# The causal mask of the encoder's scores: from a matmul into PSUM to an addition on VectorE

## The chip, the cores and the metric

One core of one Trainium2 chip runs the whole program. The metric is the device time of one execution in microseconds, here as the median of several runs. The engines are named as in the profile: PE is TensorE (PEld its weight loads), DVE is VectorE, ACT is ScalarE, POOL is GpSimd, SP is SyncE, which issues the DMAs. Each engine works through its own queue in order; semaphores hold an instruction until another engine has done its part.

## The reference

Sixteen images of 37 tokens (36 patches and one class token) of width 256 go through a patch embedding, a block of causal attention with a mixture of experts, an encoder of six layers, and a feed-forward with 4-bit rounding. The change touches the attention of the six encoder layers, of which this matters:

```python
q_pos = jnp.arange(H, T + H)[:, None]
k_pos = jnp.arange(T + H)[None, :]
delta = q_pos - k_pos
valid = (delta >= 0) & (delta <= PAST_CTX)
...
for l in range(LAYERS):
    keys = jnp.concatenate([past, x], axis=1)
    ...
    scores = jnp.einsum('bqhd,bkhd->bhqk', q, k) / jnp.sqrt(jnp.asarray(HEAD_DIM, x.dtype))
    scores = jnp.where(valid[None, None], scores, neg)
    attn = jax.nn.softmax(scores, axis=-1)
    o = jnp.einsum('bhqk,bkhd->bqhd', attn, v).reshape(B, T, C)
```

With 16 heads of 16 columns each. The feed-forward of a layer is 256 to 1024 to 256 with a gelu, and the two layer norms stand behind the two residual additions.

## The kernel before

The images are handled in two halves of eight. In the encoder the two halves run half a layer apart: a stage `phase(x, y)` does the attention of one half (x) and, woven into it, the feed-forward of the other (y). There are twelve stages with attention: first (0, 0) alone, then six with the attention of half 1 beside the feed-forward of half 0 of the same layer, and between them five with the attention of half 0 of the next layer beside the feed-forward of half 1. Below, the first is called the lone stage, the six odd, the five even. All orders are written out by hand, one queue for each engine, and semaphores tie them together.

In an attention two images share one PSUM bank as a pair: a tile of 111 rows (3 x 37 queries) by 456 columns (2 images x 2 chunks x 3 heads x 38 keys). `scores` on TensorE (L825) fills it: one bf16 product of an identity with the mask, `amask` (L834), opens the bank and writes the mask into it, and four float32 products (L841) add the scores on top. VectorE then takes `row_max` from the bank (L2138) and `shift` subtracts it, from the bank into the probability tile `Pr` in SBUF (L2142), which frees the bank (`s_shifted`). ScalarE takes the exponent in place (L1545), VectorE the row sums (L2149) and their reciprocals (L2153), GpSimd multiplies (`normalise`, L1981), and TensorE transposes the result (L855) for the product with the values.

TensorE's order in a stage with both parts is: the transposed layer norm (L755), pairs 0 and 1, the first two hidden blocks of the feed-forward (L803), pair 2, two hidden blocks (L788), pair 3, four hidden blocks, the down products (L1330, 48 of them), the four sets of transposes (L855). Six PSUM banks go round in this order, so that each job waits for the job six places ahead of it (`free_bank`): the fourth hidden block uses the bank of pair 0, pair 3 that of pair 1, the seventh hidden block that of pair 2, the second half of the down products that of pair 3.

A hidden block goes through ScalarE (gelu, L1896, twice: in full and as a rounded high part `HF_H`). Its low part `HF_L`, the difference of the two, is made by VectorE for blocks 0 to 3 (`low_hidden`, L2722, `hl_ready`) and by GpSimd for blocks 4 to 7 (L2058). The down products of a block wait for its low part, in the order of the blocks. GpSimd also splits the layer's weights in the stages with y = (0, l) (L2000).

## Time and profile before

| | |
|---|---|
| median of 3 runs | 821.11 us (820.96 to 821.4) |
| span of the profiled execution, first to last instruction | 819.1 us |
| the profiled execution's own time | not listed; the median is 2.0 us above the span |
| PE, DVE, ACT, POOL busy | 98%, 77%, 56%, 31% of the span |
| granted TensorE clock | 1.000 over the whole span |
| mask products (L834), all / in the encoder | 56 / 48 |

The busy share of PE is that of pipelined matmuls, so a record is longer than the step from one matmul to the next. Times inside a stage are read from the timeline, which gives the start of each instruction in microseconds from the start of the span, its duration, and in brackets how long its engine stood idle before it and what ended that. Instructions of the same kind are merged, with their number behind an x.

### The profile page before, as it was taken

What the parts mean: (1) busy time and instruction counts of PE and PEld (TensorE: products, weight loads), DVE (VectorE), ACT (ScalarE), POOL (GpSimd) and SP (SyncE); (2) the same over time, 40 slices, a digit from 0 to 9 for tenths busy, and PEclk for the clock granted to TensorE, in tenths of its full rate; (3) what the DMA queues carried; (4) which work ended last, traced back from release to release, by engine and by line L of the source; (5) the groups of instructions that cost most, each with busy time, mean ns of one, the idle gap of its engine ahead of it and who ended that gap; (6) DMA issues with size and microseconds to landing.
All of it is one profiled execution on the core that took longest, in us unless ns stands there. A gap on an engine that the chain in (4) does not pass through costs nothing.

```text
span 819.1 us, 16629 instructions
## 1 busy us (share of the span) xinstructions
PE 801.5 (98%) x6060; PEld 751.4 (92%) x6060; DVE 633.9 (77%) x1287; ACT 460.6 (56%) x829; POOL 251.6 (31%) x297
## 2 busy tenths in 40 slices
PE   9999999999999999999999999999999999999988
PEld 8998789999999999899999989999998999999758
DVE  5786693778778876778797887878778787876796
ACT  4386424433333336585786777667687767745421
POOL 0002120410111100364366147335525623633020
PEclk9999999999999999999999999999999999999999
DMA  5010946998889812010210021031012103010001
GB/s 191 1 52 1 373 124 253 328 323 310 317 309 337 321 53 107 1 40 14 100 44 0 17 98 38 13 102 38 4 39 72 38 13 102 26 82 1 1 0 30
DMA packets 18290, 88.36 MB, mean 108 GB/s; under 512 B 3120, under 2 KB 7472, under 8 KB 12240
## 3 DMA queue, kind: packets, MB, share of 16 engines
q1 hardware_dynamic: 18256, 87.90, 30.4%
q8 instruction: 22, 0.36, 0.2%
q14 instruction: 12, 0.10, 0.0%
HBM read 85.05 MB, written 2.84 MB: 107 GB/s over the span
## 4 chain that ended last, share of the span: by engine, by line
PE 47%; issue 23%; POOL 18%; DVE 8%; ACT 3%; DMA 1%; POOLq 0%; SPq 0%; DVEq 0%; ACTq 0%
PE bank L1139 14%; POOL W_L L2000 7%; PE bank L1176 6%; POOL HF_L L2058 4%; POOL arena L1981 3%; POOL WQKV_L L2000 3%; PE bank L746 2%; PE bank L872 2%; PE bank L1185 2%; PE bank L722 2%; PE bank L1049 2%; PE bank L788 1%; POOL SQ L2019 1%; PE bank L1123 1%; PE bank L1490 1%
## 5 line engine op out<-in xcount | busy, mean ns | idle before, releaser
L1139 PE MATMUL bank<-arena 128*128 (+1 forms) x1024 | 117.8, 274 | 0.0
L1139 PEld LDWEIGHTS bank<-arena 128*128 128x128 f32 x1024 | 117.4, 192 | 0.0
L1981 POOL TENSOR_TENSOR arena<-arena,srec 111x456 f32<-111x456 f32 x56 | 52.3, 962 | 125.1 <-DVE srec L2153 125.1
L2000 POOL TENSOR_TENSOR W_L<-LW,W_H 128x256 fp32r<-128x256 f32 x96 | 68.5, 752 | 36.9 <-DVE XHL L2589 33.5
L2058 POOL TENSOR_TENSOR HF_L<-arena,HF_H 128x296 fp32r<-128x296 f32 x48 | 43.8, 937 | 76.7 <-ACT HF_H L1896 76.7
L788 PE MATMUL bank<-XHL,W_H 128*128 128x296 f32 x288 | 65.1, 307 | 0.0
L1896 ACT ACTIVATE arena<-bank,vec 128x296 f32<-128x296 f32 x96 | 48.8, 509 | 20.4 <-PE bank L788 15.4
L2012 POOL TENSOR_TENSOR QW<-QW,arena x14 | 22.4, 1600 | 119.0 <-DVE QW L2490 65.6
L1330 PE MATMUL bank<-HF_L,W_H 128*128 128x296 f32 x192 | 57.4, 299 | 0.0
L1330 PE MATMUL bank<-HF_H,W_H 128*128 128x296 f32 x192 | 57.4, 299 | 0.0
L1330 PE MATMUL bank<-HF_H,W_L 128*128 128x296 f32 x192 | 57.3, 299 | 0.0
L872 PE MATMUL bank<-arena 114*128 114x111 f32 x448 | 55.1, 276 | 0.8 <-issue 0.7
L872 PEld LDWEIGHTS bank<-arena 114*128 114x128 f32 x448 | 53.1, 192 | 2.6 <-issue 1.3
L2165 DVE TENSOR_SCALAR OB<-bank,lvec 96x148 f32<-96x148 f32 x144 | 51.1, 368 | 5.7 <-PE bank L872 3.3
L841 PEld LDWEIGHTS bank<-arena 128*111 128x111 f32 x448 | 52.4, 175 | 1.1
L841 PE MATMUL bank<-arena 128*111 128x114 f32 x448 | 52.7, 260 | 0.0
L2149 DVE TENSOR_REDUCE ssum<-arena 111x12 f32<-111x456 f32 x56 | 32.1, 608 | 23.8 <-ACT arena L1545 23.6
L788 PEld LDWEIGHTS bank<-XHL,W_H 128*128 128x128 f32 x288 | 48.3, 188 | 0.3
L1896 ACT ACTIVATE HF_H<-bank,vec 128x296 fp32r<-128x296 f32 x96 | 48.3, 503 | 0.0
L788 PE MATMUL bank<-XHL,WQKV_H 128*128 128x296 f32 x192 | 45.4, 311 | 0.0
L2138 DVE TENSOR_REDUCE smax<-bank 111x12 f32<-111x456 f32 x56 | 33.9, 622 | 14.4 <-PE bank L841 14.3
L2497 DVE TENSOR_TENSOR EWD_L<-arena,EWD_H 128x2048 fp32r<-128x2048 f32 x16 | 36.9, 2304 | 10.0 <-ACT EWD_H L1758 10.0
(276 smaller groups left out, 2205.4 us busy)
## 6 DMA issues: line engine op xcount, KB each, us to landing
arena<-ew_in SPq DMA_DIRECT2D x16, 2048.0 KB, 9.0
arena<-ew_in SPq DMA_DIRECT2D x16, 1024.0 KB, 7.0
LW<-lw_in SPq DMA_DIRECT2D x12, 1024.0 KB, 5.0
arena<-route SPq DMA_DIRECT2D x32, 185.0 KB, 3.2
LW<-lw_in SPq DMA_DIRECT2D x6, 768.0 KB, 4.3
fp_weights<-arena SPq DMA_DIRECT2D x1, 2048.0 KB, 6.4
arena<-fp_weights SPq DMA_DIRECT2D x1, 2048.0 KB, 7.2
arena<-patches_in SPq DMA_DIRECT2D x2, 864.0 KB, 7.4
```

Of the source, the lines that this page charges most:

```text
L788: last = mm(o, w, x, start=(i == 0), stop=(i == len(pairs) - 1))
L841: last = mm(o[0:QROWS, col:col + KROWS], Qe[:, h, c, bb].rearrange("p s q -> p (s q)"), Ke[:, at_half(plan, h), c, bb].rearrange("p g k -> ...
L872: last = mm(o[:, i * QROWS:(i + 1) * QROWS], Ve[0:KROWS, at_half(plan, h) * HB + b % HB, c * P:(c + 1) * P], PTr[0:KROWS, b % PSLOTS, c, : ...
L1139: last = mm(o[:, m * CAP:(m + 1) * CAP], w[:, kc, mi * P:(mi + 1) * P], xg(kc, e), start=(kc == 0), stop=(kc == C - 1))
L1176: last = mm(bank[4][0:CAP, 0:D], hid_part, w_part, start=(m == 0 and i == 0), stop=(m == EM - 1 and i == 2))
L1330: last = mm(bank_of(plan, keys[c])[:, 0:NHALF], w, moving, start=(m == 0 and i == 0), stop=(m == FM - 1 and i == 2))
L1896: last = f(out[:, m, :], bank_of(plan, ("f1", FM * hy + m))[:, 0:NHALF], ACT.Gelu, bias=vec[:, 3 * C + m:3 * C + m + 1])
L1981: nc.gpsimd.tensor_tensor(v, v, srec[0:QROWS, s:s + 2, :].unsqueeze(3).to_broadcast([QROWS, 2, C * JH, KEYS]), ALU.mult).then_inc(p_ready, 1)
L2000: last = nc.gpsimd.tensor_tensor(low[:, cols], value[:, cols], high[:, cols], ALU.subtract)
L2058: nc.gpsimd.tensor_tensor(HF_L[:, m, :], HF[:, m, :], HF_H[:, m, :], ALU.subtract).then_inc(hl_ready_pool, 1)
L2165: return v.tensor_scalar(dst, src, bias(c)[lo:hi, :], None, ALU.add)
L2497: v.tensor_tensor(EWD_L[s][:, :, :], value, EWD_H[s][:, :, :], ALU.subtract).then_inc(wd_low, 1)
```

## The change

In the encoder (not in block 0) the mask product goes, and the first of the four score products of a pair opens the bank. VectorE gets a new step, `add_mask`: it reads the bank and the mask (in SBUF, bf16, the same for all heads) and writes the masked scores into `Pr`. It counts up a new semaphore `s_masked`, for which `free_bank` now waits in place of `s_shifted`. The max is then taken from `Pr` (`masked_max`) and subtracted in `Pr` in place (`masked_shift`). VectorE's order in the score block is written anew, and the low parts of hidden blocks 0 and 1 move inside it.

```diff
+                    if prev[0] == "s" and not plan.first:
+                        pe.wait_ge(s_masked, count_in(plan, prev, r, key) - PER_ROUND["s"])
-                    if needs is not None and needs[0] == prev[0]:
+                    elif needs is not None and needs[0] == prev[0]:
...
-                mm(o[0:QROWS, 0:2 * SCOLS], amask[:, 0:QROWS],
-                   amask[:, m0:m0 + KROWS].unsqueeze(1).to_broadcast([P, 2 * C, KROWS]), start=True, stop=False,
-                   skip_group_check=True)
+                if plan.first:
+                    mm(o[0:QROWS, 0:2 * SCOLS], amask[:, 0:QROWS],
+                       amask[:, P:P + KROWS].unsqueeze(1).to_broadcast([P, 2 * C, KROWS]), start=True, stop=False,
+                       skip_group_check=True)
...
+            def add_mask(r, plan, p):
+                dve.wait_ge(filled["s"], nth("s", p, r))
+                v.tensor_tensor(pair_probs(p).rearrange("p (x g) k -> p x (g k)", g=JH),
+                                bank_of(plan, ("s", p))[0:QROWS, 0:2 * SCOLS].rearrange("p (x n) -> p x n", n=KROWS),
+                                amask[0:QROWS, P + KROWS:P + 2 * KROWS].unsqueeze(1).to_broadcast([QROWS, 2 * C, KROWS]),
+                                ALU.add).then_inc(s_masked, 1)
+
+            def masked_max(r, p):
+                dve.wait_ge(s_masked, nth_enc("s", p, r))
+                v.tensor_reduce(pair_view(smax, p), pair_probs(p), AX.X, ALU.max).then_inc(s_max, 1)
+
+            def masked_shift(r, p):
+                dve.wait_ge(s_max, nth("s", p, r))
+                v.tensor_tensor(pair_probs(p), pair_probs(p),
+                                pair_view(smax, p).unsqueeze(2).to_broadcast([QROWS, 2 * C * JH, KEYS]), ALU.subtract
+                                ).then_inc(s_shifted, 1)
...
-                    for i in range(1, HB // 2):
-                        row_max(rx, plan, p0 + i)
-                        shift(rx, plan, p0 + i - 1)
-                        if y and i == 3:
-                            low_hidden(0, 1)
-                    shift(rx, plan, p0 + HB // 2 - 1)
+                    add_mask(rx, plan, p0)
+                    add_mask(rx, plan, p0 + 1)
+                    masked_max(rx, p0)
+                    masked_max(rx, p0 + 1)
+                    masked_shift(rx, p0)
+                    masked_shift(rx, p0 + 1)
...
```

The rest of the order can be seen in what VectorE's queue holds. The score block of a stage with both parts, before (`smax` is the tile of maxima, L2722 the low parts of hidden blocks 0 to 3):

```order
L2138 TENSOR_REDUCE smax<-bank 111x12 [waits s_psum] x2
L2142 TENSOR_TENSOR arena<-bank,smax 111x456 [waits s_max]
L2138 TENSOR_REDUCE smax<-bank 111x12 [waits s_psum]
L2142 TENSOR_TENSOR arena<-bank,smax 111x456 [waits s_max]
L2138 TENSOR_REDUCE smax<-bank 111x12 [waits s_psum]
L2142 TENSOR_TENSOR arena<-bank,smax 111x456 [waits s_max]
L2722 TENSOR_TENSOR HF_L<-arena,HF_H 128x296 [waits gelu_ready] x2
L2142 TENSOR_TENSOR arena<-bank,smax 111x456 [waits s_max]
L2722 TENSOR_TENSOR HF_L<-arena,HF_H 128x296 [waits gelu_ready] x2
L2149 TENSOR_REDUCE ssum<-arena 111x12 [waits p_exp] x2
```

And after the change, where L2142 is the masked add, L2149 the max, L2153 the shift, and L2743 the low parts:

```order
L2142 TENSOR_TENSOR arena<-bank,amask 111x456 [waits s_psum] x2
L2149 TENSOR_REDUCE smax<-arena 111x12 [waits s_masked] x2
L2153 TENSOR_TENSOR arena<-arena,smax 111x456 [waits s_max] x2
L2142 TENSOR_TENSOR arena<-bank,amask 111x456 [waits s_psum]
L2743 TENSOR_TENSOR HF_L<-arena,HF_H 128x296 [waits gelu_ready]
L2149 TENSOR_REDUCE smax<-arena 111x12 [waits s_masked]
L2142 TENSOR_TENSOR arena<-bank,amask 111x456 [waits s_psum]
L2153 TENSOR_TENSOR arena<-arena,smax 111x456 [waits s_max]
L2149 TENSOR_REDUCE smax<-arena 111x12 [waits s_masked]
L2743 TENSOR_TENSOR HF_L<-arena,HF_H 128x296 [waits gelu_ready]
L2153 TENSOR_TENSOR arena<-arena,smax 111x456 [waits s_max]
L2743 TENSOR_TENSOR HF_L<-arena,HF_H 128x296 [waits gelu_ready] x2
```

Four masked adds are new, the max and the shift read `arena` (the probability tile) and no bank, the low part of block 0 stands between the third add and the third max, that of block 1 between the fourth max and the fourth shift, and those of blocks 2 and 3 still behind all of them.

TensorE's queue around pair 3 of such a stage, before (L788 are the fourth and then the fifth hidden block):

```order
L788 MATMUL bank<-XHL,W_H 128x296 [waits s_shifted]
L788 MATMUL bank<-XHL,W_L 128x296
L788 MATMUL bank<-XHL,W_H 128x296
L788 MATMUL bank<-XHL,W_L 128x296
L788 MATMUL bank<-XHL,W_H 128x296 x2
L834 MATMUL bank<-amask 111x456 [waits s_shifted]
L841 MATMUL bank<-arena 111x114 x4
L788 MATMUL bank<-XHL,W_H 128x296 [waits gelu_ready]
```

After the change (L791 is the hidden block, L844 the score products):

```order
L791 MATMUL bank<-XHL,W_H 128x296 [waits s_masked]
L791 MATMUL bank<-XHL,W_L 128x296
L791 MATMUL bank<-XHL,W_H 128x296
L791 MATMUL bank<-XHL,W_L 128x296
L791 MATMUL bank<-XHL,W_H 128x296 x2
L844 MATMUL bank<-arena 111x114 [waits s_masked]
L844 MATMUL bank<-arena 111x114 x3
L791 MATMUL bank<-XHL,W_H 128x296 [waits gelu_ready]
```

The mask product is gone there, and the fourth hidden block and pair 3 wait for the masked add of pairs 0 and 1 and no longer for their shift.

The stage with attention alone has this on VectorE before, between the spread of the values and the row sums:

```order
L2138 TENSOR_REDUCE smax<-bank 111x12 [waits s_psum]
L2138 TENSOR_REDUCE smax<-bank 111x12 [waits s_psum,fp4_stored]
L2142 TENSOR_TENSOR arena<-bank,smax 111x456 [waits s_max]
L2138 TENSOR_REDUCE smax<-bank 111x12 [waits s_psum]
L2142 TENSOR_TENSOR arena<-bank,smax 111x456 [waits s_max]
L2138 TENSOR_REDUCE smax<-bank 111x12 [waits s_psum]
L2142 TENSOR_TENSOR arena<-bank,smax 111x456 [waits s_max] x2
L2149 TENSOR_REDUCE ssum<-arena 111x12 [waits p_exp] x2
```

After:

```order
L2142 TENSOR_TENSOR arena<-bank,amask 111x456 [waits s_psum,fp4_stored]
L2142 TENSOR_TENSOR arena<-bank,amask 111x456 [waits s_psum]
L2149 TENSOR_REDUCE smax<-arena 111x12 [waits s_masked] x2
L2153 TENSOR_TENSOR arena<-arena,smax 111x456 [waits s_max] x2
L2142 TENSOR_TENSOR arena<-bank,amask 111x456 [waits s_psum]
L2149 TENSOR_REDUCE smax<-arena 111x12 [waits s_masked]
L2142 TENSOR_TENSOR arena<-bank,amask 111x456 [waits s_psum]
L2153 TENSOR_TENSOR arena<-arena,smax 111x456 [waits s_max]
L2149 TENSOR_REDUCE smax<-arena 111x12 [waits s_masked]
L2153 TENSOR_TENSOR arena<-arena,smax 111x456 [waits s_max]
L2170 TENSOR_REDUCE ssum<-arena 111x12 [waits p_exp] x2
```

Eight instructions become twelve ahead of the first row sum (L2149 before, L2170 after).

## Rows read from the trace of the kernel before

**Rows 1.** Page, busy us (share of the span) and instructions of the engines:

```profile
PE 801.5 (98%) x6060; PEld 751.4 (92%) x6060; DVE 633.9 (77%) x1287; ACT 460.6 (56%) x829; POOL 251.6 (31%) x297
```

**Rows 2.** Line of the mask product: durations min/median/max ns; idle time before it:

```profile
L834 PE MATMUL bank<-amask x56: 353/356/402, 48.3 to 712.7; 128*111 128x456 bf16 x56
...
  DVE arena L2142: 1.3, 6
```

**Rows 3.** Timeline of TensorE (start us, duration us), odd stage, third and fourth mask:

```profile
639.28 0.35 PE L834 MATMUL bank<-amask 128*111 128x456 bf16 x1
639.48 0.94 PE L841 MATMUL bank<-arena 128*111 128x114 f32 x8
...
642.14 0.13 PEld L834 LDWEIGHTS bank<-amask 128*111 128x111 bf16 x1 [0.23 <-DVE arena L2142]
```

**Rows 4.** Timeline of VectorE, the same stage, [idle before <- what ended it]:

```profile
639.31 1.16 DVE L2138 TENSOR_REDUCE smax<-bank 111x12 f32<-111x456 f32 x2
640.39 0.62 DVE L2142 TENSOR_TENSOR arena<-bank,smax 111x456 f32<-111x456 f32 x1
...
643.36 0.63 DVE L2138 TENSOR_REDUCE smax<-bank 111x12 f32<-111x456 f32 x1 [1.27 <-PE bank L841]
...
649.49 1.16 DVE L2149 TENSOR_REDUCE ssum<-arena 111x12 f32<-111x456 f32 x2 [2.15 <-ACT arena L1545]
```

**Rows 5.** Timeline of GpSimd and VectorE, single instructions of the same stage:

```profile
638.27 4.22 POOL L2000 TENSOR_TENSOR W_L<-LW,W_H 128x256 fp32r<-128x256 f32 x6 [1.31 <-DVE XHL L2589]
...
645.17 0.83 POOL L2058 TENSOR_TENSOR HF_L<-arena,HF_H 128x296 fp32r<-128x296 f32 x1 [2.68 <-ACT HF_H L1896]
...
645.99 1.02 POOL L2058 TENSOR_TENSOR HF_L<-arena,HF_H 128x296 fp32r<-128x296 f32 x1
...
645.74 0.58 DVE L2722 TENSOR_TENSOR HF_L<-arena,HF_H 128x296 fp32r<-128x296 f32 x1
...
646.25 1.08 DVE L2722 TENSOR_TENSOR HF_L<-arena,HF_H 128x296 fp32r<-128x296 f32 x1
```

**Rows 6.** Timeline of GpSimd and VectorE, the lone stage, single instructions:

```profile
333.51 1.19 POOL L1981 TENSOR_TENSOR arena<-arena,srec 111x456 f32<-111x456 f32 x1
...
334.35 0.67 DVE L2576 TENSOR_TENSOR XD<-CN,const 128x296 f32<-128x296 f32 x1
```

**Rows 7.** Lines of VectorE: durations min/median/max ns, first and last start:

```profile
L2138 DVE TENSOR_REDUCE smax<-bank x56: 569/622/635, 49.8 to 714.0; 111x12 f32<-111x456 f32 x56
...
L2149 DVE TENSOR_REDUCE ssum<-arena x56: 568/616/628, 52.2 to 721.9; 111x12 f32<-111x456 f32 x56
...
L2722 DVE TENSOR_TENSOR HF_L<-arena,HF_H x48: 455/466/1086, 361.7 to 747.0; 128x296 fp32r<-128x296 f32 x48
```

**Rows 8.** Timeline of TensorE, odd stage, first down product and the transposes:

```profile
646.45 0.30 PE L1330 MATMUL bank<-HF_H,W_H 128*128 128x296 f32 x1
...
653.00 1.36 PE L855 MATMUL bank<-const,arena 111*114 111x111 f32 x12
654.70 0.57 PE L855 MATMUL bank<-const,arena 111*114 111x111 f32 x4 [0.34 <-POOL arena L1981]
```

**Rows 9.** Timeline of an even stage: VectorE, GpSimd, TensorE:

```profile
674.45 1.16 DVE L2138 TENSOR_REDUCE smax<-bank 111x12 f32<-111x456 f32 x2
...
680.32 3.62 POOL L2058 TENSOR_TENSOR HF_L<-arena,HF_H 128x296 fp32r<-128x296 f32 x4 [12.13 <-ACT HF_H L1896]
...
681.58 0.31 PE L1330 MATMUL bank<-HF_H,W_H 128*128 128x296 f32 x1
```

**Rows 10.** Timeline of the lone stage: VectorE, GpSimd:

```profile
326.54 0.63 DVE L2138 TENSOR_REDUCE smax<-bank 111x12 f32<-111x456 f32 x1 [0.30 <-PE bank L841]
...
330.33 1.15 DVE L2149 TENSOR_REDUCE ssum<-arena 111x12 f32<-111x456 f32 x2
...
331.69 4.14 POOL L1981 TENSOR_TENSOR arena<-arena,srec 111x456 f32<-111x456 f32 x4 [37.17 <-DVE srec L2153]
```

More of the change, by code:

```diff
@@ L430, in build @@
         q_ready, k_ready, v_ready, o_ready = (sem(n) for n in ("q_ready", "k_ready", "v_ready", "o_ready"))
+        s_masked = sem("s_masked")
         s_max, s_shifted, p_exp, s_sum, s_rec, p_ready, pt_ready = (
@@ L832, in scores @@
                 o = bank_of(plan, key)
-                m0 = P + (0 if plan.first else KROWS)
-                mm(o[0:QROWS, 0:2 * SCOLS], amask[:, 0:QROWS],
-                   amask[:, m0:m0 + KROWS].unsqueeze(1).to_broadcast([P, 2 * C, KROWS]), start=True, stop=False,
-                   skip_group_check=True)
+                if plan.first:
+                    mm(o[0:QROWS, 0:2 * SCOLS], amask[:, 0:QROWS],
+                       amask[:, P:P + KROWS].unsqueeze(1).to_broadcast([P, 2 * C, KROWS]), start=True, stop=False,
+                       skip_group_check=True)
                 for i in range(2):
@@ L841, in scores @@
                         last = mm(o[0:QROWS, col:col + KROWS], Qe[:, h, c, bb].rearrange("p s q -> p (s q)"),
-                                  Ke[:, at_half(plan, h), c, bb].rearrange("p g k -> p (g k)"), start=False, stop=True,
+                                  Ke[:, at_half(plan, h), c, bb].rearrange("p g k -> p (g k)"),
+                                  start=not plan.first and i + c == 0, stop=True,
                                   skip_group_check=True)
@@ L2752, in phase @@
                 if x:
-                    row_max(rx, plan, p0)
                     if isinstance(lx, int) and hx + lx == 0:
                         dve.wait_ge(fp4_stored, 32)
-                    for i in range(1, HB // 2):
-                        row_max(rx, plan, p0 + i)
-                        shift(rx, plan, p0 + i - 1)
-                        if y and i == 3:
-                            low_hidden(0, 1)
-                    shift(rx, plan, p0 + HB // 2 - 1)
+                    add_mask(rx, plan, p0)
[4 more added lines that the diff above has]
+                    masked_shift(rx, p0 + 1)
+                    add_mask(rx, plan, p0 + 2)
+                    if y:
+                        low_hidden(0)
+                    masked_max(rx, p0 + 2)
+                    add_mask(rx, plan, p0 + 3)
+                    masked_shift(rx, p0 + 2)
+                    masked_max(rx, p0 + 3)
+                    if y:
+                        low_hidden(1)
+                    masked_shift(rx, p0 + 3)
                     if y:
```

## The prediction

> **What bounds the kernel now.** I read the page first: TensorE is busy 98% of the span and VectorE 77% [rows 1]. So a matmul that goes is worth its slot, as long as nothing else then comes late. Next the mask product's own line: 56 of them, 356 ns each by the record, and a wait of 1.3 us in 6 cases for the shift of an earlier pair [rows 2]. The change keeps 8 of the 56 (block 0) and removes 48, four in each of twelve encoder stages: one lone, six odd, five even. Then the timeline of one odd stage: the score block on VectorE has a hole of 1.27 us ahead of the fourth max and one of 2.15 us ahead of the first row sum [rows 4]. That looks like room for the added work. The question is whether the rest of VectorE's queue, the low parts of the hidden blocks above all, still comes in time for TensorE.
>
> **What is removed.** Matmuls overlap, so the price is the step to the next start and not the 356 ns: 639.28 to 639.48, 0.20 us [rows 3]. Four make 0.80 us a stage; in odd stages the fourth score pair also waited 0.23 us for a shift [rows 3], which goes because the bank is now free at the masked add. So TensorE reaches its down products 1.03 us earlier in an odd stage and 0.8 us in an even one. Were that all, 6 x 1.03 + 6 x 0.8 = 11 us would go.
>
> **What is added on VectorE.** Four masked adds a stage, from PSUM with a mask in SBUF. No row shows one; the nearest are the shift from PSUM, 0.62 us also while GpSimd runs [rows 4], and the max and the row sum of the same size, 0.622 and 0.616 us [rows 7]. Back to back they start 0.54 us apart (two maxima from 639.31, the next instruction at 640.39 [rows 4]). I take 0.54; the bounds are 0.5 and 0.65. So max from SBUF costs what it cost from PSUM, and the block grows by 4 x 0.54 = 2.2 us.
>
> The Trainium skill, "VectorE: DVE Perf Modes", section on the TRN2 errata, gives 58 cycles of fixed cost from SBUF and 120 from PSUM, so max and shift would each be shorter by an estimated 0.065 us. The 0.616 beside 0.622 us do not show it [rows 7]. By the page the third shift would be issued some 0.3 us earlier, the even stages would lose nothing (see the race below) and the sum would be about 825.
>
> **The shift changes its kind.** It now reads two tensors in SBUF, as the low parts of L2722 do. Those take 0.46 us alone and up to 1.09 us [rows 7]. The row by row view says why: one is issued at 645.74 while GpSimd's first low part runs (645.17 to 646.00) and ends at 646.32; the next is issued at 646.25 and ends at 647.33, 0.32 us behind the end of GpSimd's second, which itself took 1.02 instead of 0.83 us [rows 5]. So the two take turns, whole instruction by whole instruction. An addition with a repeated second operand is held in the same way: issued at 334.35, it ends at 335.02, 0.32 us behind GpSimd's 333.51 + 1.19 [rows 6]. For 456 columns I scale: a held shift ends 0.32 x 456/296 = 0.49 us after GpSimd's instruction, and pushes the next one back by 0.19 + 0.17 = 0.36 us.
>
> The Trainium skill, "SBUF — State Buffer", section "SBUF: two separate sides", states this as an exclusive lock between GpSimd and VectorE instructions with two SBUF inputs. By it the masked shift is held and the masked add and the max are not; by that rule the trace agrees for two other operations [rows 5, 6]; none shows it for the shift itself.
>
> **An odd stage, worked out** (the times are those of the stage shown [rows 4]). Masked adds at 639.31 and 639.85, max at 640.39 and 640.93, first shift issued at 641.47. GpSimd splits weights until 642.49 in six of 0.70 us [rows 5]: the shift waits for the fifth (641.8) and ends at 642.3, the sixth moves to 642.87, the second shift ends at 643.36. Third add to 643.9, low part 0 to 644.28, third max, fourth add, third shift issued at 645.28. GpSimd's low parts, which follow the hidden blocks, start at 645.17 - 1.03 = 644.15 and end at 645.05 and 645.85, so the third shift ends at 646.34. Fourth max, low part 1 issued at 646.8: held by GpSimd's third (to 647.1), done at 647.4. Fourth shift held by GpSimd's fourth (to 648.1), done at 648.6. Low parts 2 and 3 at 648.95 and 649.35.
> TensorE: the seventh hidden block needs the bank of the third pair, masked at 643.9, and would start at 646.45 - 12 x 0.137 - 1.03 = 643.78, so it loses some 0.2 us; down starts at 646.45 - 1.03 + 0.2 = 645.6 (48 products in the 6.55 us to 653.00, 0.137 us each, 0.82 us a hidden block [rows 8]). Block 1 is wanted at 646.4 and its low part comes at 647.4: 1.0 us of waiting. Block 2 is wanted at 648.2, ready at 648.95: 0.75 us. Block 3 is in time. The transposes start at 653.00 - 0.83 + 1.75 = 653.9 instead of 653.00. Before, the fourth set waited for GpSimd's normalised tile and began at 654.70 [rows 8]; now the row sum starts at 649.4 (649.49 before [rows 4]), so that tile is no later and there is nothing to wait for: the fourth set begins some 1.2 us behind the first, 655.1. **Odd: +0.4 us each.**
>
> **An even stage.** GpSimd splits nothing in the score block. First add at 674.45 [rows 9], third shift issued at 679.68. GpSimd's low parts start at 680.32 - 0.8 = 679.52, so they win by 0.16 us. Shift to 680.84, low part 1 to 681.8, fourth shift to 683.0, low part 2 to 683.95. Down starts at 681.58 - 0.8 = 680.78 [rows 9]; block 1 waits 0.25 us, block 2 1.35 us. The transposes come 0.8 us later, the fourth set, relieved of its wait of about 0.5 us, **+0.3 us each**. If the shift won that race, low part 2 would be ready at some 683.4 and the stage would lose nothing.
>
> **The lone stage.** Here no feed-forward covers anything. VectorE runs without a pause from its second max (326.54, behind a hole of 0.30 us) to the row sum (330.33), and GpSimd, which releases the transposes, waits for it until 331.69 [rows 10]. Four more instructions less the hole: 4 x 0.54 - 0.3 = **+1.9 us**, all on the path. No GpSimd work stands beside it, so no shift is held.
>
> **Sum.** 1.9 + 6 x 0.4 + 5 x 0.3 = +5.8 us in the profiled execution, whose span is 819.1; the runs' median is 821.11, 2.0 above the span, and so what lies around the span is taken as unchanged and the difference is added to the median: 826.9. Bounds: no loss in even stages and 0.2 in odd ones gives +3.1 (824.2); 0.6 in both gives +8.5 (829.6).
>
> **The rivals.**
> *Faster: the ports do not hold the masked shift* (or GpSimd lets it by). Then low part 1 is ready before TensorE wants it and the waits in down vanish; the fourth transposes move with the gelus, by 1.0 us a stage: 11 x -1.0 + 1.9 = -9.1 us, 812. It decides from the point where low part 1 is done before 646.2 in the odd stage. For it: the shift from PSUM was never held [rows 4]. Against it: two instructions that were held, one with a repeated operand [rows 5, 6]. A part of it, low part 2 held but not 1, gives about 0.4 us less a stage than before, 817 to 819.
> *No change:* the even stages win the race and gain a little, the odd ones break even, and the lone stage alone is left: 821.1 + 1.9 less one or two, 821 to 822.7.
> *Much slower:* the low parts slip by one more GpSimd instruction (0.8 us) in every stage: 826.9 + 11 x 0.5 = 832.4.
>
> **How the numbers follow.** A measurement tells 0.2% (1.6 us) from no change. Forecast, 823 to 830: 0.58. Much slower: 0.07. Within 0.2%: 0.14. Faster: 0.21, of which 0.11 near 812 and 0.10 between 815 and 819. So faster 0.21, same 0.14, slower 0.65. The range for 8 in 10 leaves out the case near 812 and the far end above: 815 to 831; the forecast's own range is 823 to 830.
>
> **What would show it.** In the changed profile: 8 mask products on TensorE; masked shifts of about 0.6 us alone but 0.8 to 1.2 us beside GpSimd; TensorE waiting in the down products for HF_L of VectorE, about 1.7 us a stage; no wait of the fourth transposes for GpSimd; the lone stage's row sums 1.9 us later. I am wrong if shifts beside GpSimd stay at 0.62 us, or if no wait for HF_L appears in down.

## The result, and the profile after

The changed kernel takes 825.97 us (825.26 to 826.4, 4 runs) against 821.13 us before (820.96 to 821.4, 4 runs, the same chip): a ratio of 1.0054, 95% interval 1.004 to 1.0069. It is slower by 4.8 us; 826.9 was forecast.

The page's line of the engines, as [rows 1]. TensorE has 48 matmuls and 4.0 us of work less, VectorE 48 instructions and 28.8 us more:

```profile
PE 797.5 (97%) x6012; PEld 746.9 (91%) x6012; DVE 662.7 (80%) x1335; ACT 459.7 (56%) x829; POOL 260.6 (32%) x297
```

The new lines of VectorE and the low parts, as [rows 7] (durations min/median/max in ns, first and last start, forms). L2142 is the masked add, L2149 the max, L2153 the masked shift, L2743 the low part:

```profile
L2142 DVE TENSOR_TENSOR arena<-bank,amask x48: 618/623/630, 326.6 to 720.2; 111x456 f32<-111x456 f32 x48
...
L2149 DVE TENSOR_REDUCE smax<-arena x48: 614/617/628, 327.7 to 721.9; 111x12 f32<-111x456 f32 x48
...
L2153 DVE TENSOR_TENSOR arena<-arena,smax x48: 621/1116/1249, 328.8 to 722.9; 111x456 f32<-111x456 f32 x48
...
L2743 DVE TENSOR_TENSOR HF_L<-arena,HF_H x48: 450/455/546, 365.0 to 752.4; 128x296 fp32r<-128x296 f32 x48
```

Add and max hardly vary (by 12 and 14 ns). The shift does: 0.62 us at best, 1.12 in the median. The low parts, up to 1086 ns before [rows 7], are now at most 546: the shifts have taken over being held.

What TensorE waits for, in all (us, times, longest), on its weight loads first and then on the matmuls:

```profile
PEld bank L1334 <- DVE HF_L L2743: 15.5, 22, 1.1
```

```profile
PE bank L1334 <- DVE HF_L L2743: 9.6, 17, 0.9
PE bank L859 <- POOL arena L1985: 2.8, 2, 2.4
```

The first row is the new loss: the down products wait for VectorE's low parts, twice in each of the 11 stages that have them. It is read on the weight loads, because a matmul's record (0.30 us) is longer than the step to the next (0.137): the bracket behind a matmul begins at the end of that record and so shows less than was lost. The last row is the lone stage.

The odd stage, as [rows 4 and 5]: VectorE, then GpSimd (start, duration, xcount):

```profile
643.95 1.16 DVE L2142 TENSOR_TENSOR arena<-bank,amask 111x456 f32<-111x456 f32 x2
645.02 1.15 DVE L2149 TENSOR_REDUCE smax<-arena 111x12 f32<-111x456 f32 x2
646.09 1.94 DVE L2153 TENSOR_TENSOR arena<-arena,smax 111x456 f32<-111x456 f32 x2
...
649.95 1.10 DVE L2153 TENSOR_TENSOR arena<-arena,smax 111x456 f32<-111x456 f32 x1
650.98 0.62 DVE L2149 TENSOR_REDUCE smax<-arena 111x12 f32<-111x456 f32 x1
651.51 0.54 DVE L2743 TENSOR_TENSOR HF_L<-arena,HF_H 128x296 fp32r<-128x296 f32 x1
651.98 1.24 DVE L2153 TENSOR_TENSOR arena<-arena,smax 111x456 f32<-111x456 f32 x1
653.14 0.83 DVE L2743 TENSOR_TENSOR HF_L<-arena,HF_H 128x296 fp32r<-128x296 f32 x2
```

```profile
643.61 3.94 POOL L2004 TENSOR_TENSOR W_L<-LW,W_H 128x256 fp32r<-128x256 f32 x5
648.91 1.65 POOL L2062 TENSOR_TENSOR HF_L<-arena,HF_H 128x296 fp32r<-128x296 f32 x2 [1.36 <-ACT HF_H L1900]
650.74 1.98 POOL L2062 TENSOR_TENSOR HF_L<-arena,HF_H 128x296 fp32r<-128x296 f32 x2 [0.18 <-ACT HF_H L1900]
```

VectorE goes without a pause, but part of that is time in which GpSimd holds it: the third shift, issued at 649.95, ends at 651.05, 0.49 us behind GpSimd's second low part (650.56). The low part of block 1 comes at 652.05. TensorE's matmuls and weight loads of that stage, as [rows 8]:

```profile
650.38 0.30 PE L1334 MATMUL bank<-HF_H,W_H 128*128 128x296 f32 x1
...
658.66 1.68 PE L859 MATMUL bank<-const,arena 111*114 111x111 f32 x16
```

```profile
652.11 0.19 PEld L1334 LDWEIGHTS bank<-HF_H,W_H 128*128 128x128 f32 x1 [0.99 <-DVE HF_L L2743]
...
653.65 0.19 PEld L1334 LDWEIGHTS bank<-HF_H,W_H 128*128 128x128 f32 x1 [0.69 <-DVE HF_L L2743]
```

Block 1 waits 0.99 us and block 2 0.69; the down products take 658.66 - 650.38 = 8.28 us instead of 6.55 [rows 8]. All four sets of transposes then run as one group (x16), without the wait for GpSimd of [rows 8].

The even stage, as [rows 9]: VectorE, GpSimd's four low parts and the last two of them alone, TensorE's two waits and its transposes:

```profile
684.75 1.17 DVE L2153 TENSOR_TENSOR arena<-arena,smax 111x456 f32<-111x456 f32 x1
...
686.38 0.55 DVE L2743 TENSOR_TENSOR HF_L<-arena,HF_H 128x296 fp32r<-128x296 f32 x1
686.85 1.25 DVE L2153 TENSOR_TENSOR arena<-arena,smax 111x456 f32<-111x456 f32 x1
688.02 0.83 DVE L2743 TENSOR_TENSOR HF_L<-arena,HF_H 128x296 fp32r<-128x296 f32 x2
```

```profile
684.61 4.93 POOL L2062 TENSOR_TENSOR HF_L<-arena,HF_H 128x296 fp32r<-128x296 f32 x4 [11.35 <-ACT HF_H L1900]
...
686.56 1.04 POOL L2062 TENSOR_TENSOR HF_L<-arena,HF_H 128x296 fp32r<-128x296 f32 x1
...
687.57 1.97 POOL L2062 TENSOR_TENSOR HF_L<-arena,HF_H 128x296 fp32r<-128x296 f32 x1
```

```profile
686.98 0.19 PEld L1334 LDWEIGHTS bank<-HF_H,W_H 128*128 128x128 f32 x1 [0.36 <-DVE HF_L L2743]
...
688.53 0.19 PEld L1334 LDWEIGHTS bank<-HF_H,W_H 128*128 128x128 f32 x1 [0.70 <-DVE HF_L L2743]
```

```profile
693.54 1.69 PE L859 MATMUL bank<-const,arena 111*114 111x111 f32 x16
```

GpSimd wins the first race (684.61 against 684.75), as forecast. But its fourth low part, issued at 687.57 while the fourth shift is at work, takes 1.97 us: VectorE's low parts 2 and 3, next in its queue, go ahead of it, and low part 2 is done at 688.47. It was the other way round just before: the fourth shift was issued as closely behind low part 1 (at 686.85, with low part 1 ending at 686.93), and yet GpSimd's third low part (issued at 686.56, done at 687.60) came in between them, so that the shift ended at 688.10.

The lone stage, as [rows 10]: TensorE's first two sets of transposes, and its granted clock (the column behind the engines' busy times):

```profile
335.70 0.60 PE L859 MATMUL bank<-const,arena 111*114 111x111 f32 x4 [2.40 <-POOL arena L1985]
336.71 0.85 PE L859 MATMUL bank<-const,arena 111*114 111x111 f32 x4 [0.41 <-POOL arena L1985]
```

```profile
336.00:338.00 2.00, 1.59 (x11) 1.41 (x9) 1.93 (x6) 0.45 (x1) 2.00 (x3) 0.71 0.00 0
338.00:340.00 2.00, 2.00 (x12) 2.00 (x11) 1.54 (x3) 1.74 (x4) 0.84 (x1) 0.50 0.00 0
```

TensorE stands idle for 2.40 us, and behind that the clock falls to 0.50, the lower of its two levels (1.2 of 2.4 GHz), where it was 1.00 throughout before.

By stage, counted from the last transpose of one stage to the last of the next, and for the lone stage from its first score product (mask or score) to the first product with the values:

| us | before | after | difference | forecast |
|---|---|---|---|---|
| lone stage | 12.13 | 15.13 | +3.0 | +1.9 |
| odd stages, median of six | 35.58 | 36.00 | +0.4 (sum +2.4) | +0.4 (+2.4) |
| even stages, all five | 35.12 | 34.89 | -0.23 (sum -1.15) | +0.3 (+1.5) |

Together +4.25 us. The profiled execution also reached its first score product 1.0 us later. That is scatter: in the traces below, of kernels that leave the front of the program alone, that product starts between 324.5 and 325.4 us.

### The profile page after: what moved, and what is told of

It reads as the page before. It is cut to its first block, busy times and chain, and to the rows that moved or that the text cites. A ratio compares the mean times of both kernels' runs of the same rounds, so it can differ in the third digit from the quotient of the medians.

```text
span 824.5 us, 16651 instructions
## 1 busy us (share of the span) xinstructions
PE 797.5 (97%) x6012; PEld 746.9 (91%) x6012; DVE 662.7 (80%) x1335; ACT 459.7 (56%) x829; POOL 260.6 (32%) x297
## 4 chain that ended last, share of the span: by engine, by line
PE 62%; DVE 21%; issue 9%; POOL 5%; ACT 2%; DMA 1%; DVEq 0%; SPq 0%; POOLq 0%; ACTq 0%
PE bank L1143 14%; PE bank L1334 7%; PE bank L1180 6%; DVE arena L2153 3%; PE bank L747 3%; DVE smax L2149 3%; PE bank L791 3%; POOL W_L L2004 2%; PE bank L859 2%; PE bank L876 2%; DVE arena L2122 2%; PE bank L723 2%; PE bank L824 2%; PE bank L894 2%; DVE OB L2186 2%
## 5 line engine op out<-in xcount | busy, mean ns | idle before, releaser
L2004 POOL TENSOR_TENSOR W_L<-LW,W_H 128x256 fp32r<-128x256 f32 x96 | 70.9, 775 | 37.8 <-DVE XHL L2610 33.5
L2062 POOL TENSOR_TENSOR HF_L<-arena,HF_H 128x296 fp32r<-128x296 f32 x48 | 50.5, 1068 | 66.0 <-ACT HF_H L1900 65.9
L1334 PE MATMUL bank<-HF_H,W_H 128*128 128x296 f32 x192 | 59.7, 311 | 10.2 <-DVE HF_L L2743 9.6
L791 PE MATMUL bank<-XHL,W_H 128*128 128x296 f32 x288 | 65.8, 308 | 0.0
L844 PE MATMUL bank<-arena 128*111 128x114 f32 x448 | 51.2, 262 | 0.0
L1334 PEld LDWEIGHTS bank<-HF_H,W_H 128*128 128x128 f32 x192 | 36.1, 188 | 15.5 <-DVE HF_L L2743 15.5
L1566 ACT ACTIVATE arena<-bank 114x444 f32<-114x444 f32 x56 | 26.2, 544 | 42.0 <-PE bank L859 42.0
L791 PEld LDWEIGHTS bank<-XHL,W_H 128*128 128x128 f32 x288 | 48.3, 188 | 0.9 <-DVE arena L2142 0.8
L844 PEld LDWEIGHTS bank<-arena 128*111 128x111 f32 x448 | 48.4, 175 | 0.8
L2023 POOL TENSOR_TENSOR SQ<-SQ 128x296 f32<-128x296 f32 x24 | 19.6, 815 | 86.5 <-ACT SQ L1538 86.5
L2153 DVE TENSOR_TENSOR arena<-arena,smax 111x456 f32<-111x456 f32 x48 | 46.1, 979 | 0.0
```

Source lines behind the costliest of these rows:

```text
L791: last = mm(o, w, x, start=(i == 0), stop=(i == len(pairs) - 1))
L844: last = mm(o[0:QROWS, col:col + KROWS], Qe[:, h, c, bb].rearrange("p s q -> p (s q)"), Ke[:, at_half(plan, h), c, bb].rearrange("p g k -> ...
L1334: last = mm(bank_of(plan, keys[c])[:, 0:NHALF], w, moving, start=(m == 0 and i == 0), stop=(m == FM - 1 and i == 2))
L2004: last = nc.gpsimd.tensor_tensor(low[:, cols], value[:, cols], high[:, cols], ALU.subtract)
L2062: nc.gpsimd.tensor_tensor(HF_L[:, m, :], HF[:, m, :], HF_H[:, m, :], ALU.subtract).then_inc(hl_ready_pool, 1)
L2153: v.tensor_tensor(pair_probs(p), pair_probs(p), pair_view(smax, p).unsqueeze(2).to_broadcast([QROWS, 2 * C * JH, KEYS]), ALU.subtract).the ...
```

## The experiments

Theory: GpSimd's low parts hold the masked shift because both its operands are now in SBUF, and VectorE's low parts, queued behind it, come too late. Rivals: the four added instructions cost this by themselves; or TensorE's relief was worth less than its slots. The runs are compared with runs of the kernel before on the same chip (821.3 to 821.6 us).

| run | us | ratio to before, 95% |
|---|---|---|
| max in PSUM | 815.06 | 0.9905 to 0.9938 |
| gap ahead of low part 2 | 828.68 | 1.0075 to 1.0109 |
| mask on both engines | 826.0 | 1.004 to 1.0074 |
| max in PSUM, lone stage on TensorE | 812.31 | 0.9875 to 0.9908 |
| the same, mask on both engines | 819.95 | 0.9973 to 0.9992 |
| masked add written into PSUM | 831.41 | 1.0107 to 1.0141 |
| low parts first | 824.75 | 1.0025 to 1.0059 |
| lone stage on TensorE | 823.11 | 1.001 to 1.003 |
| 40 constant products | 825.88 | 1.0035 to 1.0069 |
| 33 constant products | 825.32 | 1.003 to 1.0064 |
| max in PSUM, lone on TensorE, reciprocals sooner | 809.22 | 0.9836 to 0.9869 |
| kernel before, reciprocals sooner | 817.9 | 0.9941 to 0.9975 |

**Is it the hold?** The max goes to spare PSUM columns, so that the shift has one operand in SBUF; order, adds and TensorE's work stay.

```diff
+            def max_at(p):
+                return bank[6 + p % 2][0:QROWS, 484 + 12 * (p // 2 % 2):496 + 12 * (p // 2 % 2)]
...
-                v.tensor_reduce(pair_view(smax, p), pair_probs(p), AX.X, ALU.max).then_inc(s_max, 1)
+                v.tensor_reduce(max_at(p), pair_probs(p), AX.X, ALU.max).then_inc(s_max, 1)
...
                 v.tensor_tensor(pair_probs(p), pair_probs(p),
-                                pair_view(smax, p).unsqueeze(2).to_broadcast([QROWS, 2 * C * JH, KEYS]), ALU.subtract
+                                max_at(p).unsqueeze(2).to_broadcast([QROWS, 2 * C * JH, KEYS]), ALU.subtract
```

> The changed kernel, but the masked max is written to twelve spare PSUM columns and the masked shift reads it there, so that the shift has one operand in SBUF instead of two. Theory (the shift is held by GpSimd because both its operands are in SBUF): shifts take 0.62 us beside GpSimd too, the low parts come about 0.8 to 1.2 us sooner in odd stages, the waits for them in the down products go, 1.2 us an odd and 0.46 us an even stage: 826.0 - 7.2 - 2.3 = 816.5 us, 815.5 to 818.5. Rival (the four added instructions are the cost, not the hold): 825 to 826.5, with shifts still at 0.8 to 1.2 us, or shorter with the same waits in down.

815.06 us, 10.9 less than the changed kernel. The shift's line in that kernel, and what is left of TensorE's waits for VectorE's low parts (us, times, longest):

```profile
L2156 DVE TENSOR_TENSOR arena<-arena,bank x48: 616/622/629, 327.9 to 711.3; 111x456 f32<-111x456 f32 x48
```

```profile
PEld bank L1334 <- DVE HF_L L2746: 0.8, 5, 0.2
```

No shift is stretched, and on the weight loads the waits for `HF_L` fall from 15.5 us to 0.8. Odd stages take 34.65 us and even ones 34.37, 0.93 and 0.75 below the kernel before. In these eleven stages the hold is the cause of the loss, and the added instructions are not: all 48 adds are still there. The lone stage, where nothing was held, keeps its loss (14.85 us, 2.7 more than before).

The Trainium skill, "SBUF — State Buffer", section "SBUF: two separate sides", says that a VectorE instruction with two SBUF inputs and a GpSimd instruction that reads SBUF lock each other out for a whole instruction. By that rule the trace agrees: 1116 ns in the median with two such inputs, 622 with one, for the same tile and neighbours.

**The even stage.** One tiny instruction between the fourth shift and low part 2, so that VectorE's next instruction with two operands in SBUF does not stand right behind the shift:

```diff
                     masked_shift(rx, p0 + 3)
                     if y:
+                        v.memset(gap[:, :], 0.0)
                         low_hidden(2, 3)
```

> The changed kernel with one tiny VectorE instruction (a constant written into 128 x 1 elements that nothing reads) between the fourth masked shift and low part 2 in the odd and even stages. Theory (in even stages low part 2 comes ahead of GpSimd's fourth low part because VectorE issues it right behind the held shift, before the port passes on): with the gap GpSimd's fourth runs first, low part 2 ends some 0.75 us later, TensorE's wait for it grows from 0.46 to 1.2 us, and each even stage is 0.6 to 0.8 us longer, odd ones unchanged or up to 0.1 longer: 826.0 + 3.5 = 829.5 us. Rival (the order of the two does not hang on that): only the tiny instruction's own step, 0.05 to 0.1 us a stage, 826.0 to 827.2 us.

828.68 us, 2.7 more than the changed kernel. Even stages take 35.48 us, 0.59 more; odd ones 36.01, no more than in the changed kernel (one of the six 36.16). The even stage, VectorE, GpSimd's fourth and TensorE's wait for block 2:

```profile
688.65 1.24 DVE L2154 TENSOR_TENSOR arena<-arena,smax 111x456 f32<-111x456 f32 x1
689.83 1.06 DVE L2744 TENSOR_TENSOR HF_L<-arena,HF_H 128x296 fp32r<-128x296 f32 x1
689.84 0.06 DVE L2794 MEMSET gap<- 128x1 f32 x1
```

```profile
689.37 1.19 POOL L2063 TENSOR_TENSOR HF_L<-arena,HF_H 128x296 fp32r<-128x296 f32 x1
```

```profile
690.94 0.19 PEld L1335 LDWEIGHTS bank<-HF_H,W_H 128*128 128x128 f32 x1 [1.31 <-DVE HF_L L2744]
```

Now GpSimd's fourth goes first (1.19 us instead of 1.97), low part 2 is held for 1.06 us, and TensorE waits 1.31 us for it. All five even stages go this way. So behind the fourth shift the tiny instruction is enough to change who comes next. Why is not shown: its record starts 0.01 us behind that of low part 2, so the rows give no length for the pause, and an instruction of VectorE that stands ready does not always go first, as GpSimd's third low part shows in the rows of the even stage above. With the gap an even stage costs 0.36 us more than before, close to the +0.3 that the prediction gave it.

**What was the relief of TensorE worth?** The mask product back on TensorE as well, first in the changed kernel, then where nothing is held:

```diff
-                if plan.first:
+                if True:
+                    m0 = P + (0 if plan.first else KROWS)
                     mm(o[0:QROWS, 0:2 * SCOLS], amask[:, 0:QROWS],
-                       amask[:, P:P + KROWS].unsqueeze(1)...
+                       amask[:, m0:m0 + KROWS].unsqueeze(1)...
...
-                                  start=not plan.first and i + c == 0, stop=True,
+                                  start=False, stop=True,
```

> The changed kernel, and the mask product back on TensorE as well in all twelve encoder stages (the mask is then added twice, which leaves the same probabilities). It prices what the change took from TensorE with VectorE's new block in place. Theory: in odd stages TensorE only arrives later at a low part for which it waits 1.2 us anyway, and in even ones at a wait of 0.46, so little is lost: 0.1 to 0.3 us an odd stage, 0.3 to 0.5 an even one, 828 to 830 us. Rival (the stage is bound by TensorE throughout, the waits being in slack): 12 x 0.80 = +9.6, 835.6 us.

826.0 us, the same as without: less than either expectation. Even stages lose 0.18 us (35.07); odd ones gain 0.17 (35.83). In the odd stage TensorE, some 0.45 us later at its down products, waits 0.36 and 0.70 us there instead of 0.99 and 0.69, as it does in the even stages of the changed kernel (its rows, then VectorE's low parts 2 and 3 and GpSimd's fourth):

```profile
651.16 0.19 PEld L1335 LDWEIGHTS bank<-HF_H,W_H 128*128 128x128 f32 x1 [0.36 <-DVE HF_L L2744]
...
652.71 0.19 PEld L1335 LDWEIGHTS bank<-HF_H,W_H 128*128 128x128 f32 x1 [0.70 <-DVE HF_L L2744]
```

```profile
652.21 0.83 DVE L2744 TENSOR_TENSOR HF_L<-arena,HF_H 128x296 fp32r<-128x296 f32 x2
```

```profile
651.75 1.97 POOL L2063 TENSOR_TENSOR HF_L<-arena,HF_H 128x296 fp32r<-128x296 f32 x1
```

A later TensorE makes later gelus, so GpSimd's low parts fall later into VectorE's block, and here too its fourth lets low parts 2 and 3 by. Over the eleven stages that is -0.7 + 0.9, next to nothing. The equal medians hide a little: two of the four executions had a granted clock of 1.000 in the mean of the span (825.42 and 825.54 us) and two 0.998 (826.46 and 826.7), as all four of the changed kernel had. At 0.998 the products cost some 0.6 us, by two executions against four.

> The kernel with the max in PSUM and the lone stage's mask on TensorE (812.3 us), with the mask product back on TensorE in the odd and even stages as well (there the mask is added twice). It prices the removal on TensorE where no low part is late. Theory (a matmul that goes is worth its slot only where TensorE then finds its operands): 4 x 0.20 us in each of 11 stages, 812.3 + 8.8 = 821.1 us, 819 to 822, whereas in the changed kernel the same products cost nothing (826.0 with, 826.0 without). Rival (TensorE's slot is worth little here too, the rest of the gain being VectorE's): 812.5 to 815 us.

819.95 us, 7.6 more than without the products, 0.69 a stage; odd stages go from 34.66 to 35.31, even ones from 34.35 to 35.06. Where the low parts are in time a mask product is worth nearly its 0.20 us; behind a held shift it is worth next to nothing.

**Two other ways around the hold.** The masked add back into its own PSUM bank, with max and shift from PSUM as before the change, so that the bank comes free at the shift again:

```diff
-                    if prev[0] == "s" and not plan.first:
-                        pe.wait_ge(s_masked, count_in(plan, prev, r, key) - PER_ROUND["s"])
-                    elif needs is not None and needs[0] == prev[0]:
+                    if needs is not None and needs[0] == prev[0]:
...
-                v.tensor_tensor(pair_probs(p).rearrange("p (x g) k -> p x (g k)", g=JH),
+                v.tensor_tensor(bank_of(plan, ("s", p))[0:QROWS, 0:2 * SCOLS].rearrange("p (x n) -> p x n", n=KROWS),
...
-                v.tensor_tensor(pair_probs(p), pair_probs(p),
+                v.tensor_tensor(pair_probs(p), score_view(plan, p),
...
```

> The changed kernel, but the masked add writes back into its own PSUM bank; max and shift read PSUM as before the change, and the bank comes free at the shift again. So VectorE has the same four added instructions and TensorE the same relief, without a shift that reads two tensors in SBUF. Theory (the hold by GpSimd is what costs): no shift is stretched beside GpSimd, the waits for low parts in the down products go, and the time is near that of the kernel with the max in PSUM, 815.1 us, plus what the later release of the banks costs in score pairs and hidden blocks (0 to 0.5 us a stage): 815 to 821 us. Rival (the earlier release of the banks was most of that gain): 824 us or more.

831.41 us: a miss. No shift is held (622 to 633 ns), but TensorE waits for the banks (all such waits on the weight loads and on the matmuls, then one):

```profile
PEld bank L789 <- DVE arena L2151: 16.6, 11, 1.6
```

```profile
PE bank L789 <- DVE arena L2151: 13.9, 11, 1.3
```

```profile
650.38 0.40 PE L789 MATMUL bank<-XHL,W_H 128*128 128x296 f32 x1 [1.32 <-DVE arena L2151]
```

That is the fourth hidden block, which uses the bank of pair 0; the shift that frees it now stands behind two adds and two maxima. So what I had put at 0 to 0.5 us costs 1.5 in every stage (16.6 / 11), and in this order of VectorE's work it is the early release at the masked add that keeps TensorE from waiting for the longer block. Another order was not tried.

The other way leaves the shift as it is and takes the low parts ahead of the third and fourth:

```diff
-                    masked_shift(rx, p0 + 2)
+                    if y:
+                        low_hidden(1)
                     masked_max(rx, p0 + 3)
                     if y:
-                        low_hidden(1)
+                        low_hidden(2)
+                    if y:
+                        low_hidden(3)
+                    masked_shift(rx, p0 + 2)
                     masked_shift(rx, p0 + 3)
-                    if y:
-                        low_hidden(2, 3)
```

> The changed kernel with another order on VectorE alone: the low parts 1, 2 and 3 stand ahead of the third and fourth masked shifts. Theory (TensorE loses its time to low parts that stand behind held shifts): the waits in down shrink from 0.75 + 0.45 us in an odd and 0.46 in an even stage to nearly nothing, 0.5 to 0.9 us an odd and 0.2 to 0.4 an even stage come back, 826.0 - 4.2 - 1.5 = 820.3 us, 819 to 822. Rival (the shifts, now some 1.5 us later, delay the row sums and GpSimd's normalised tiles, for which the transposes then wait): 824 us or more, with waits of the transposes for GpSimd in every stage.

824.75 us, 1.2 less, near the rival. The waits for `HF_L` are gone, but the late shifts delay the row sums and GpSimd's tiles, for which the transposes then wait twice a stage (an odd stage):

```profile
657.25 0.56 PE L859 MATMUL bank<-const,arena 111*114 111x111 f32 x4 [0.34 <-POOL arena L1985]
658.38 0.56 PE L859 MATMUL bank<-const,arena 111*114 111x111 f32 x4 [0.57 <-POOL arena L1985]
```

Odd stages gain 0.3 us, even ones lose 0.25. An order of the same held work moves the wait and removes little of it.

**The lone stage.** First back to TensorE's mask in this stage alone:

```diff
-                if plan.first:
+                on_pe = plan.first or plan is PHASE[0, None]
+                if on_pe:
...
+                    if not y:
+                        row_max(rx, plan, p0)
...
+                            shift(rx, plan, p0 + i - 1)
```

> The changed kernel, but the lone stage alone has its mask product on TensorE, and its max and shift from PSUM, as before the change. Theory: the lone stage costs the changed kernel 3.1 us (1.9 of VectorE's path and some 1.2 of a TensorE clock that fell after its idle stretch), so this gives 826.0 - 3.1 = 822.9 us, and the granted clock stays at 1.00 in that stage. Rival (the 3.1 us belong to the front of that one profiled run, or come back later): 825 to 826.5.

823.11 us, 2.9 less, and the stage takes 12.13 us, as before the change, at a clock of 1.00. Then, with the masked add left in place, more constant products ahead of the transposes, so that TensorE isn't idle:

```diff
-                        transpose_probs(rx, plan, p0 + i, 0 if y else (21, 0, 2, 2)[i])
+                        transpose_probs(rx, plan, p0 + i, 0 if y else (40, 2, 2, 2)[i])
```

> The changed kernel, with 40 instead of 21 constant products ahead of the lone stage's first transposes and 2 instead of none ahead of its second, so that TensorE does not stand idle for 2.4 us there. Theory: the granted clock stays at 1.00 through 336 to 342 us, the transposes take 0.57 instead of 0.85 to 0.95 us, and about 1.2 us come back: 824.8 us. Rival (the stage is late for VectorE and GpSimd alone, the clock costs nothing): 826.0 us, with the clock at 1.00 all the same.

825.88 us: the clock stayed at 1.00, but 40 products last until 337.0 us, so the transposes began 12.07 us behind the stage's first score product instead of 10.39, and the stage took 14.98 us. With 33:

> As the kernel with 40 constant products ahead of the lone stage's first transposes, which kept the granted clock at 1.00 but kept TensorE itself busy until 337.00, 1.3 us past the 335.70 at which the transposes began in the changed kernel: with 33 they end at about 335.6. Theory (the fall of the clock costs the lone stage some 1.2 us): the way from the first score to the end of the last transposes is 13.7 instead of 15.0 us, and 826.0 - 1.2 = 824.8 us. Rival (the clock costs nothing that the wait for GpSimd's tiles does not cost anyway): 14.7 to 15.1 us, 826.0 us.

The transposes begin 10.51 us behind it, nearly as in the changed kernel, and the stage takes 14.16 us, 0.97 less; the clock in its last 4 us (column behind the engines):

```profile
336.00:338.00 2.00, 1.91 (x19) 1.73 (x17) 1.93 (x5) 0.45 (x1) 2.00 (x3) 1.00 0.00 0
338.00:340.00 2.00, 1.92 (x17) 1.56 (x15) 1.49 (x2) 1.99 (x5) 0.79 (x1) 1.00 0.00 0
```

The runs give 825.32 us, 0.65 less than the changed kernel, which is too little for four runs to tell; so the clock's price stands by the trace. It agrees with the mean clocks of single executions: in four of the kernels here that leave TensorE idle in this stage some executions had 1.000 and others 0.998, and those at 1.000 were shorter by 0.4 to 1.1 us (one to three executions on each side). It agrees too with the kernel whose masked add is written into PSUM: there TensorE was idle for 2.42 us, the clock happened to stay at 1.00, and the stage took 14.17 us. So the lone stage's +3.0 us in the profiled run are 2.0 of VectorE's path and 1.0 of the clock.

**A version faster than both.** Max in PSUM and the lone stage's mask on TensorE:

> Masked max in PSUM (815.1 us) together with the lone stage's mask product on TensorE as before the change (worth 2.9 us in the changed kernel). Theory (the two losses are separate places, one held shift per covered stage and one bare path): they add, 815.1 - 2.9 = 812.2 us. Rival (what the lone stage gives back is taken again by the waits for GpSimd's normalised tiles that stand in the kernel with the max in PSUM): 814 to 815 us.

812.31 us: the two add up. First on TensorE's list is now the wait of the transposes for GpSimd's tiles:

```profile
PE bank L861 <- POOL arena L1987: 2.7, 12, 0.3
```

The chain of four tiles begins with the first reciprocal, so this goes ahead of the second row sum:

```diff
-                    for i in range(0, HB // 2, 2):
-                        row_sum(rx, p0 + i)
-                        row_sum(rx, p0 + i + 1)
-                        row_recip(rx, p0 + i)
-                        row_recip(rx, p0 + i + 1)
+                    row_sum(rx, p0)
+                    row_recip(rx, p0)
+                    row_sum(rx, p0 + 1)
+                    row_recip(rx, p0 + 1)
...
```

> The kernel with the max in PSUM and the lone stage's mask on TensorE (812.3 us), with the first two reciprocals each right behind its row sum instead of behind both row sums. Theory (what is left is the wait of the fourth transposes for GpSimd's chain of four normalised tiles, 0.16 to 0.3 us in 12 stages, 2.7 us in all): the chain starts some 0.4 us sooner, these waits go, 812.3 - 2.4 = 809.9 us, 809.5 to 811. Rival (the two reciprocals, each now behind a wait for its sum, push the later row sums and reciprocals back by as much): 812 to 813 us.

809.22 us, 12.1 below the kernel before, and that row is gone. The step by itself, in the kernel before:

> The kernel before the change, with only the sooner reciprocals (the step that took the kernel with the max in PSUM from 812.3 to 809.2 us). Theory (that step belongs to GpSimd's chain of tiles and is to be had without the change): before the change the fourth transposes wait 0.3 to 0.5 us in 11 stages, so 821.3 - 3.5 = 817.8 us, 817 to 819.5, and the masked add on VectorE with its max in PSUM is still worth 8 to 9 us. Rival (the step pays only where VectorE's block is the longer one): 820.5 to 821.5 us.

817.9 us: 3.4 of the 12.1 us belong to that step, which needs no change of the mask. The mask on VectorE without the hold, in the eleven stages with both parts, is worth the other 8.7.

## Why the prediction was right, and where it was not

The time was 0.9 us off, but two of its terms were off by more and offset each other, so that the closeness is in part luck.

- **The odd stage: right in each step.** TensorE reaches its down products 0.74 us earlier (26.29 instead of 27.03 us into the stage; 0.83 forecast), waits 0.99 and 0.69 us (1.0 and 0.75), starts the transposes 1.0 us later (0.9), and the wait of the fourth set for GpSimd is gone, as forecast. The stage is 0.4 us longer, as forecast. One small slip did not matter: the prediction gave GpSimd's first two low parts 1.70 us, where the row of 0.83 each makes 1.66 and 1.65 was measured.
- **What is added: right.** Two masked adds take 645.02 - 643.95 = 1.07 us, 0.54 each. Max from SBUF is 617 ns in the median and was 622 from PSUM [rows 7]. The fixed costs that the Trainium skill gives apart ("VectorE: DVE Perf Modes", TRN2 errata) don't show in these two figures. The sum of about 825 that went with them came within 1.0 us, but not by its step, the third shift winning the race of the even stage: it lost it (684.75 against 684.61).
- **The shift is held: right**, also in size: the third shift of the odd stage ended 0.49 us behind GpSimd's low part, as estimated. The rival that it isn't held was told apart: with one operand in PSUM the kernel takes 815.06 us, and 812.31 with the lone stage repaired as well. That rival's sum of 812 had a lone stage of 1.9 us in it, where 2.7 were paid in that trace.
- **The even stage: wrong.** GpSimd won the race, TensorE came 0.76 us earlier (0.8 forecast), and block 1 waited 0.36 us (0.25). The failed step is "fourth shift to 683.0, low part 2 to 683.95", which let GpSimd's fourth low part in between. VectorE's next instruction went first: block 2 waited 0.70 us instead of 1.35, and the stage gained 0.23 us instead of losing 0.3. Why it went first here, when GpSimd's third low part had come between low part 1 and the fourth shift as forecast, stays open. With the gap it waited 1.31 us and lost 0.36. Five stages: 2.65 us too much.
- **The lone stage: mechanism right, size too small.** The row sum starts 8.02 us behind the first score product instead of 6.00, so 2.0 later where 1.9 was forecast. But I priced the stage at a full clock: TensorE, idle for 2.40 us, got half a clock for its transposes, another 1.0 us.
- **The sum:** 1.1 us too little in the lone stage, 2.65 too much in the even ones, 5.8 forecast, 4.25 by the stages and 4.8 by the medians.
- **Much slower** did not come: no low part slipped by the further GpSimd instruction that it needed, for the waits were 0.99 and 0.69 us in odd stages (1.0 and 0.75 forecast) and less in even ones.

## What to carry to other kernels

Where work moves from TensorE to VectorE, look at how many SBUF operands its neighbours are left with: a step that read PSUM and now reads SBUF twice can lose more, through GpSimd, than the moved work costs. A slot on the bounding engine is worth its time only if its next operands are in time as well (here 0.69 us a stage or next to nothing, for the same four products); and a stage that nothing covers is best left as it was. Price each stage kind by itself: the same edit cost 3.0 us in one, 0.4 in six and gained 0.23 in five.

## What the runs showed of the hardware that I had not expected

- When a GpSimd instruction and a VectorE instruction with two operands in SBUF both wait for a third to end, they do not simply take turns. Behind the fourth shift VectorE's low part 2 went first in all five even stages, and GpSimd's low part took 1.97 us instead of 0.82. Behind low part 1, with the fourth shift issued as closely, GpSimd's went first in all eleven stages, as it did between two low parts in the kernel before [rows 5]. With a 0.06 us instruction written between the fourth shift and low part 2 GpSimd's went first there too. What decides was not settled.
- Behind 2.40 us without work TensorE's granted clock fell to 0.50 in four traces, among them that of the changed kernel, where it was 1.00 again by 342 us. In a fifth with 2.42 us it stayed at 1.00, as it did in one with 1.96. The mean clocks of the executions differ within one kernel too: 0.998 in three and 1.000 in one with the max in PSUM. What decides between them was not settled.
